# Linear attention with an FFN on one core: the running state kept as one matrix that is updated chunk by chunk, in place of prefix sums made at once

## The reference, cut to what matters

```
q, k = phi(proj(Wq, bq)), phi(proj(Wk, bk));  v = proj(Wv, bv)      # phi(x) = elu(x) + 1
def step((S, z), (qi, ki, vi)):                                     # one chunk of 128 tokens, each head
    scores = where(mask, qi @ ki.T, 0)
    num = scores @ vi + qi @ S                                      # S: 16 x 16 for each head
    den = sum(qi * (cumsum(ki) + z))
    S, z = S + ki.T @ vi, z + sum(ki)
    return num / den
```

## Time and profile before

| | |
|---|---|
| median of 3 runs | 1584.21 us (1583.21 to 1586.20) |
| the profiled execution's own time | 1583.21 us |
| its span | 1581.5 us |
| TensorE busy | 97% of the span |
| VectorE, ScalarE, GpSimd busy | 78%, 75%, 52% |
| granted TensorE clock, mean | 0.991 of 2.4 GHz |
| one batch in the loop (509.50 to 556.93 us) | 47.43 us |

### The profile page before, as it was taken

How to read it: one execution, slowest core, us unless ns; L and a number is a source line. 1 busy time by engine, 2 the same in 40 slices (tenths; PEclk the granted TensorE clock), 3 DMA queues, 4 the chain that set the end, 5 groups by cost and what they waited for, 6 DMA issues and landing times.

```text
span 1581.5 us, 41041 instructions
## 1 busy us (share of the span) xinstructions
PE 1538.9 (97%) x14820; PEld 1314.4 (83%) x14820; DVE 1230.4 (78%) x2459; ACT 1180.0 (75%) x2045; POOL 825.7 (52%) x594
## 2 busy tenths in 40 slices
PE   5799999999999999999999999999999999999997
PEld 4578888888888888888888888888888888888886
DVE  6678787878787878787878787878787878787865
ACT  3497777797777797777797777797777787777763
POOL 3255445555445555445555445555445555446553
PEclk9899999999999999999999999999999999999998
DMA  7756765546764546664557665556664446764540
GB/s 182 176 129 148 172 156 130 130 124 151 172 159 122 126 131 152 172 170 113 123 130 154 172 150 131 124 129 157 172 161 117 127 126 159 172 160 114 118 102 28
DMA packets 153944, 222.96 MB, mean 141 GB/s; under 512 B 20032, under 2 KB 71488, under 8 KB 153920
## 3 DMA queue, kind: packets, MB, share of 16 engines
q1 hardware_dynamic: 152560, 222.63, 57.4%
q10 hardware_dynamic: 1360, 0.01, 0.0%
HBM read 138.69 MB, written 83.89 MB: 141 GB/s over the span
## 4 chain that ended last, share of the span: by engine, by line
PE 89%; DVE 4%; ACT 2%; issue 2%; DMA 2%; SPq 1%; POOL 0%; DVEq 0%; ACTq 0%
PE ring L322 34%; PE num L489 8%; PE ring L384 8%; PE sc L447 7%; PE ring L385 7%; PE sc L322 5%; PE num L456 4%; PE state_acc L322 3%; PE num L322 3%; DVE probs L607 3%; PE ring L521 2%; PE state_acc L470 2%; ACT silu_f L851 1%; PE num L504 1%; PE num L384 1%
## 5 line engine op out<-in xcount | busy, mean ns | idle before, releaser
L999 POOL TENSOR_TENSOR s_lo<-silu_f,s_hi 128x512 fp32r<-128x512 f32 x256 | 341.0, 1338 | 346.8 <-ACT s_hi L862 346.8
L693 DVE SCALAR_TENSOR_TENSOR silu_f<-ring,scale,silu_f 128x512 f32<-128x512 f32 x222 | 166.3, 749 | 165.6 <-ACT silu_f L851 164.0
L322 PE MATMUL ring<-w_hi,s_hi 128*128 128x256 f32 x992 | 281.3, 284 | 0.7 <-issue 0.7
L322 PE MATMUL ring<-w_hi,s_lo 128*128 128x256 f32 x992 | 278.0, 280 | 0.0
L322 PE MATMUL ring<-w_lo,s_hi 128*128 128x256 f32 x992 | 278.0, 280 | 0.0
L607 DVE TENSOR_TENSOR probs<-sc,causal 128x512 f32<-128x512 f32 x384 | 250.6, 680 | 11.3 <-PE sc L447 7.3
L1019 POOL TENSOR_TENSOR qk<-qk,phi_q 128x512 f32<-128x512 f32 x64 | 82.7, 1292 | 265.5 <-DVE qk L660 265.5
L447 PE MATMUL sc<-q_stack,k_stack 96*128 96x256 f32 x1024 | 189.5, 302 | 12.9 <-DVE probs L607 5.5
L322 PEld LDWEIGHTS ring<-w_hi,s_hi 128*128 128x128 f32 x992 | 186.7, 188 | 14.5 <-issue 13.2
L384 PE MATMUL ring<-gt_hi,w_q 128*128 128x512 f32 x441 | 193.2, 438 | 0.0
L1006 POOL TENSOR_TENSOR probs<-probs,causal 128x512 f32<-128x512 f32 x128 | 165.6, 1294 | 46.8 <-ACT probs L944 46.8
(11 more groups left out here) (188 smaller groups left out, 3889.2 us busy)
## 6 DMA issues: line engine op xcount, KB each, us to landing
k_stack<-k_rows SPq DMA_DIRECT2D x192, 256.0 KB, 4.0
q_stack<-q_rows SPq DMA_DIRECT2D x384, 128.0 KB, 6.0
k_rows<-silu_f SPq DMA_DIRECT2D x128, 256.0 KB, 3.7
q_rows<-probs SPq DMA_DIRECT2D x128, 256.0 KB, 4.1
x_in<-in_x SPq DMA_DIRECT2D x32, 512.0 KB, 7.7
xb<-in_x SPq DMA_DIRECT2D x32, 512.0 KB, 7.3
out<-clip SPq DMA_DIRECT2D x64, 256.0 KB, 7.1
silu_f<-in_q SPq DMA_DIRECT2D x2, 512.0 KB, 9.6
```

Of the source, the lines that this page charges most:

```text
L322: last = e.matmul(target, a, b, start=(n == 0), stop=(n == 3 * len(pairs) - 1))
L693: f_b.done(e.scalar_tensor_tensor(out=slot, in0=ffn_bank(j, 1, A)[:, :], scalar=scale_1[:, 1, j:j + 1], in1=slot, op0=ALU.mult, op1=ALU.add))
L999: sl.done(e.tensor_tensor(s_lo[:, j, :], silu_f[:, j % SLOTS, :], s_hi[:, j, :].bitcast(F32), ALU.subtract))
```

## The change

`update_states` becomes `update_state(u)`, one matmul of 128 by 128 columns for each of the six steps that a later step reads (c < 3), which adds k_tok(c).T @ v(c) of all 8 heads of a half onto one 128 by 128 matrix in `state_acc`. Behind each, VectorE's `snapshot(u)` multiplies this matrix (128 columns) by `head_ones` into one of three slots of a new tile `state`. The next update waits for the snapshot before it (`snap`, now six events, as `upd_pe`). `update_state(0)` stands ahead of `fc1(2)`, the others behind `scores(u)`; `from_state(u-1)` moves ahead of `values(u-1)`. `num_pe` goes, `av_pe` of the half's last step takes its place. `den_rows` is now two slots of `state`, and `k_tok` has no second use.

```diff
-        upd_pe, snap = ev("upd_pe", 1), ev("snap", T)
-        num_pe = ev("num_pe", T)
+        upd_pe, snap = ev("upd_pe", T * (C - 1)), ev("snap", T * (C - 1))
...
-                for t in range(T):
-                    for c in range(C - 1):
-                        later = C - 1 - c
-                        for pair in range(HT // 2):
-                            rows = slice(32 * pair, 32 * pair + 32)
-                            last = e.matmul(
-                                state_sums(t)[rows, 32 * c:32 * (C - 1)].rearrange("p (n a x) -> p n a x", n=later, a=2),
-                                k_tok[:, c, t * P + 32 * pair:t * P + 32 * pair + 32],
-                                v_pad[:, c, t * HT // 2 + pair, 0:4:3, :][:, None, :, :].to_broadcast([P, later, 2, HD]),
-                                start=(c == 0), stop=True, skip_group_check=True)
-                upd_pe.done(last)
+            def update_state(u):
+                t, c = divmod(u, C)
+                if c == C - 1:
+                    return
+                n = t * (C - 1) + c
+                w.need(kt_sb, 0, c // 2)
+                w.need(v_sb, 0, max(c, 1))
+                if n:
+                    w.need(snap, 0, n - 1)
+                upd_pe.done(e.matmul(state_acc[:, t * P:(t + 1) * P], k_tok[:, c, t * P:(t + 1) * P],
+                                     v_pad[:, c, t * HT // 2:(t + 1) * HT // 2, 0:4:3, :],
+                                     start=(c == 0), stop=True, skip_group_check=True))
...
+            if A:
+                update_state(0)
             fc1(2)
             if A:
                 scores(1)
-                update_states()
+                update_state(1)
                 values(0)
...
                 if A:
                     scores(u)
+                    update_state(u)
+                    from_state(u - 1)
                     values(u - 1)
-                    from_state(u - 1)
...
-            def snapshots(t):
+            def snapshot(u):
...
+                w.need(upd_pe, 0, n)
+                if n >= 3:
+                    reader_t, reader_c = divmod(n - 3, C - 1)
+                    w.need(av_pe, 0, reader_t * C + reader_c + 1)
+                else:
+                    w.need(av_pe, -1)
+                snap.done(e.tensor_tensor(state[:, n % 3, :], state_acc[:, t * P:(t + 1) * P], head_ones[:, :], ALU.mult))
...
                 if A:
                     mask(u)
-                    if u == 3:
-                        snapshots(1)
+                    snapshot(u)
```

More of the change, by code:

```diff
@@ L141, in build @@
         probs = [sb(f"probs{n}", [P, HT, P]) for n in range(2)]
-        den_rows = sb("den_rows", [P, 2 * P])
+        state = sb("state", [P, 3, P])
         gt_hi, gt_lo = sb("gt_hi", [P, T, S], F32R), sb("gt_lo", [P, T, S], F32R)
@@ L185, in qk_bank @@
             return sc[is_q] if m else ring_bank("kq"[is_q] + "0")
-        state = k_tok[:, :, :].rearrange("p c (a x) -> p (c a) x", a=2)
-        def state_sums(t):
-            return state_acc[:, t * (C - 1) * 32:(t + 1) * (C - 1) * 32]
+        den_rows = state[:, 0:2, :].rearrange("p n x -> p (n x)")
         def den_tok(t):
@@ L454, in from_state @@
                 if c:
[L455 to L464, removed]
-                for t in range(T):
-                    for c in range(C - 1):
-                        later = C - 1 - c
-                        for pair in range(HT // 2):
-                            rows = slice(32 * pair, 32 * pair + 32)
-                            last = e.matmul(
-                                state_sums(t)[rows, 32 * c:32 * (C - 1)].rearrange("p (n a x) -> p n a x", n=later, a=2),
-                                k_tok[:, c, t * P + 32 * pair:t * P + 32 * pair + 32],
-                                v_pad[:, c, t * HT // 2 + pair, 0:4:3, :][:, None, :, :].to_broadcast([P, later, 2, HD]),
-                                start=(c == 0), stop=True, skip_group_check=True)
-                upd_pe.done(last)
+                    n = t * (C - 1) + c - 1
+                    w.need(snap, 0, n)
+                    e.matmul(num[t][:, c * P:(c + 1) * P], state[:, n % 3, :], phi_q[:, t, c * P:(c + 1) * P],
+                             start=False, stop=False, skip_group_check=True)
+            def update_state(u):
[10 more added lines that the diff above has]
+                                     start=(c == 0), stop=True, skip_group_check=True))
             def values(u):
@@ L577, in pe_iteration @@
             if A:
+                from_state(U - 1)
                 values(U - 1)
-                from_state(U - 1)
             project_kq(1)
@@ L646, in features @@
                 w.need(qk_exp, s, n)
-                w.need(num_pe, s - 1, m)
+                w.need(av_pe, s - 1, m * C + C - 1)
                 dst = phi_q if is_q else phi_k
@@ L722, in attention @@
                 w.need(rb_sb, 0, t)
-                w.need(num_pe, 0, t)
+                w.need(av_pe, 0, t * C + C - 1)
                 attn.done(e.tensor_tensor(qk[:, t, :], num[t][:, :], qk[:, t, :], ALU.mult))
@@ L760, in ve_iteration @@
             ffn_sum(1)
+            if A:
+                snapshot(0)
             ffn_sum(2)
@@ L763, in ve_iteration @@
                 mask(1)
-                snapshots(0)
+                snapshot(1)
             for u in range(2, U):
@@ L924, in ac_iteration @@
                     w.need(kt_pe, 0, n)
-                    w.need(num_pe, -1)
+                    w.need(upd_pe, -1)
                     kt_sb.done(e.activation(k_tok[:, 2 * n:2 * n + 2, :],
@@ L982, in ac_iteration @@
                 w.need(den_pe, 1)
-                den_sb.done(e.activation(den_rows[:, :], num[1][:, 0:2 * P], ACT.Copy))
+                den_sb.done(e.activation(den_rows, num[1][:, 0:2 * P], ACT.Copy))
         def po_norm(e, w, s):
```

## The result

The changed kernel takes 1602.43 us (median of 4 runs, 1601.24 to 1603.95) against 1584.03. The ratio is 1.0119, 95% interval 1.0107 to 1.0133: slower by 1.2%. The forecast was 1605, with 1594 to 1615 as its range. A batch of the loop takes 48.17 us, mean of 27 batches from the first matmul of v to the next, against 47.49 before; 48.1 was forecast. 32 x 0.68 is 21.8 us, about the 21.4 by which the two profiled spans differ (1602.9 and 1581.5); the medians differ by 18.4, and from one execution to the next the times vary by 1 to 3 us.

What follows compares the result with a forecast made beforehand. TensorE was taken as the bound (89% of the chain). Shifts of 0.44 and 0.20 us made 0.64, taken as 0.65 a batch: 20.8 us over 32 batches on 1583.2, 1604.0, median 1605, range 1594 to 1615.

Steps and rivals of the forecast that it cites:

- The cost of an update: TensorE's time for one new 128 by 128 matmul: 0.22 us, bounds 0.14 below and 0.33 above.
- R2: Rival: weight loads shown, each update costs 0.33 us; 37 us slower, 1622; chance 0.11 together with late snapshots.
- Place 1: update_state(0) ahead of fc1(2): its 0.22 us fills a wait of 0.17, leaving a shift of about 0.05.
- Places 2 and 3: Ahead of scores(2): 0.70 us of old sums go, update_state(1) adds 0.22; waiting for mask 1 spends the gain.
- Place 4: Updates 2, 4, 5 and 6 add 0.88 us; waits absorb part, mask 6 moves 0.44, leaving a shift of 0.44.
- (c): TensorE's wait for a mask ahead of scores(6): weight loads idle 0.35 us, half counted, 0.17.
- Place 5: Snapshot 6 between mask 6 and xt_lo delays the first projection record by 0.20 us; shift becomes 0.64.
- The total: TensorE's added time over a whole batch, taken as 0.65 us, 20.8 us over 32 batches.
- Edits priced at nothing: Snapshots other than the sixth, from_state ahead of values, av_pe for num_pe, and k_tok free earlier: no cost expected.
- R1: Rival: waits swallow more, because snapshot 6 doesn't bind or ScalarE doesn't slip; 14 or 8 us, 1592 to 1598; chance 0.13.
- (d): TensorE's wait at scores(7), 0.46 us over, its second half waiting for mask 6; expected to give only in part.
- R3: Rival: masks, not ScalarE, pace steps 2 to 7, shorter snapshots help; 9 us faster, 1575; chance 0.06.

Runs made afterwards that it cites:

- spare_fc2: Changed kernel with two spare matmuls of an update's form between fc2(0) and fc2(1); 1616.05 us, ratio 1.0198 to the kernel before.
- narrow_updates: Changed kernel with the updates of steps 2, 4, 5 and 6 streaming 32 columns in place of 128; 1602.08 us.
- spare_step1: Changed kernel with two spare matmuls of an update's form ahead of update_state(1); 1604.01 us.
- few_sums: Kernel before with only the first four of its 24 narrow matmuls of the state sums; 1586.04 us, ratio 0.9994.
- after_xt_early: Changed kernel with x_transposes of step 6 moved between from_state(5) and values(5); 1602.81 us.
- no_late_updates: Changed kernel without the updates of steps 2, 4, 5 and 6, snapshots and order kept; 1589.32 us.
- snap6_narrow: Changed kernel with snapshot 6 alone cut from 128 to 8 columns; 1604.60 us.
- spare_step5: Changed kernel with two spare matmuls of an update's form ahead of update_state(5); 1618.68 us.
- masks_first: Kernel before with from_state ahead of values and, in steps 1, 5 and 6, VectorE's mask ahead of ffn_sum; 1574.49 us, ratio 0.9930.
- from_state_first: Kernel before with from_state ahead of values and av_pe for num_pe; 1590.49 us, ratio 1.0031.

## Why the prediction was right, step by step

- **The cost of an update, 0.22 us.** Right: 0.22 from start to start in steps 2, 4 and 6, and 0.21 to 0.22 by spare_fc2. The weights aren't shown (R2 falls). In narrow_updates a quarter of the streamed columns, with all 128 stationary ones kept, took the same 0.54 us for update and `from_state`. The Trainium skill (TensorE: Matmul & The Clock Gate, "LDWEIGHTS (loading the stationary operand)") says that a weight load's time goes by its columns. In the trace of the kernel before a load record of 128 columns lasts 188 ns in the mean and one of 32 columns 110 ns, so more columns take longer, but not in proportion; no run varied the stationary columns of an update.
- **Place 1.** Right. The wait at `fc1(2)` is gone; `scores(1)` starts 8.20 us into the batch, 8.19 before.
- **Places 2 and 3.** Right, and the step with the best evidence: +0.44 ahead of `scores(2)` (spare_step1) and -0.52 there (few_sums) moved the batch by 0.01 and 0.08 us, and of the 0.08 all but 0.02 lies behind the projections. `update_state(1)` waited about 0.1 us for its snapshot, at no cost.
- **Place 4.** Right. The four updates add 0.22 each, (c) gave its share, and mask 6 moved by the 0.44 that was forecast: from the batch's start it is 532.67 - 509.50 = 23.17 before and 539.09 - 515.48 = 23.61 after. The second half of `scores(7)`, which waits for it, starts 0.43 later. TensorE's shift was 0.60 at the transposes and fell: `from_state(6)` and `values(6)` would have ended at 541.08 + 0.57 = 541.65, that is 26.17 into the batch, against 25.75 before. That is 0.42.
- **Place 5.** Right in size and in its chain, but it missed a second chain. `xt_lo` starts 25.02 us into the batch, 24.37 before, later by 0.65; 0.44 from mask 6 and 0.20 from the snapshot make 0.64. TensorE waits 541.84 - 541.65 = 0.19 for it, so the shift at the projections is 0.61, for 0.64. In after_xt_early and in no_late_updates this chain holds `xt_lo` alone. What I didn't see is that TensorE is 0.60 late at the transposes too, and ScalarE's `xt_hi` with them: it starts at 24.39 in place of 23.72. Without the snapshot `xt_lo` would have had to wait for it just as long (snap6_narrow). That the chain through `xt_hi` ended within 0.02 us of the forecast one, and not later, is luck. In spare_step5 it ends 0.2 later, and places 4 and 5 alone would have given too little.
- **The distance of 2.67 us** from the transposes to the projections is no proof of what the projections hang on. It is 2.66 or 2.67 in the kernel before, in the changed one and in seven more, but in masks_first and spare_step5 the transposes' chain sets it, and in the kernel before the projections don't wait for `xt_lo` at all. It is 2.73, 2.75, 2.92, 3.17 and 3.31 in the other five. The expectation of spare_step5 has it as 2.67 in every version; that is wrong.
- **The total.** 0.68 us a batch for 0.65: 0.60 ahead of the projections in the mean, and 0.08 behind them, where the forecast had nothing. There the same matmuls stand 118.7 ns apart in the changed kernel and in 12 of the 27 batches of the kernel before, and 117.3 in the other 15. I have no cause for that, and by the batches of the kernel before it need not be the change. The forecast of 48.1 for the batch started from 47.43, one of the 15; the mean is 47.49.
- **Edits priced at nothing.** `from_state` ahead of `values` is not free on the kernel before (+0.27, of which 0.19 lies ahead of the projections); what it is worth inside the changed kernel was not tried. The snapshots fit into idle time, as said.
- **R1** falls: ScalarE slipped as forecast, and the wait ahead of the projections gave back 0.19 of what (d) had absorbed. Even with snapshot 6 cut down the batch stayed (snap6_narrow). **R3** said that the masks pace steps 2 to 7. That falls for this change, but it had a grain of truth: masks queued behind a waiting `ffn_sum` cost 0.63 us a batch (masks_first against from_state_first).

## What to carry to other kernels

Price added work by where it stands, not by the engine's load alone: ahead of a wait that hangs on another engine, half a microsecond more or less of TensorE's work changed nothing; behind it the same matmuls counted in full. To find what a later wait hangs on, follow each chain that can release it, and look at its last operation: it either starts without a gap behind its engine's own work, or waits for another engine. An equal distance between two events in several versions proves little, because earlier work moves both; only a version that shortens one chain alone tells. And where two chains end together, take both away before calling either harmless.

## What the runs showed of the hardware that I had not expected

A float32 matmul with 128 stationary columns cost the same next to another such one whether it streamed 128 or 32 columns, 0.54 us for the pair. The 48 narrow records that the change removed took 0.70 us, 15 ns each, in four groups of 32 columns side by side; the wide form needs a quarter of the records and nearly twice the time, 6 x 0.22 = 1.32 us.
